# A Swin block on one core: normalized tokens transposed by SyncE's transfers, dense tokens, maxima in a row-maximum bank, first scores later

## The reference, cut to what matters

```
xn  = layernorm(x) * g1 + b1
xw  = roll(xn, (-3, -3)) cut into 7x7 windows              # 1024 windows of 49 tokens
q, k, v = xw @ qkv_w + qkv_b                               # per head
p   = softmax(q * 8**-0.5 @ k.T + position_bias + window_mask)
x1  = x + roll back((p @ v) @ proj_w + proj_b)
out = x1 + gelu(layernorm(x1) * g2 + b2 @ fc1_w + fc1_b) @ fc2_w + fc2_b
```

## Time and profile before

| | |
|---|---|
| timed runs, median | 1094.67 us |
| profiled execution | 1094.25 us, span 1092.5 us |
| attention stage, about | 55 to 833 us of the span |
| MLP stage, about | 853 to 1092 us of the span |
| busy, share of the span | PE 87%, DVE 82%, ACT 71%, POOL 69% |
| mean granted TensorE clock | 0.988 of full speed |

### The profile page before, as it was taken

One profiled execution on the slowest core, in us unless ns is written; L12 is line 12 of the kernel. 1 busy time (PEld: TensorE's weight loads), 2 busy tenths in 40 slices (PEclk: granted clock), 3 DMA queues, 4 the chain that ended last, 5 costly groups with the idle time before them and its releaser, 6 DMA issues. The chain is left out here.

```text
span 1092.5 us, 45511 instructions
## 1 busy us (share of the span) xinstructions
PE 946.4 (87%) x16004; PEld 750.9 (69%) x16004; DVE 891.7 (82%) x2021; ACT 773.7 (71%) x1733; POOL 751.6 (69%) x971
## 2 busy tenths in 40 slices
PE   0489999999999999999999999999983688888887
PEld 0268887888788878887888788887873355554555
DVE  5678888888888888888888888898975677777776
ACT  0368888888888888888888888888863444444544
POOL 6258888888888888888888888888865444444441
PEclk9999999999999999999999999999996899999999
DMA  1022222222222222222222222232220343444444
GB/s 54 22 72 74 67 74 72 64 65 75 73 62 65 74 72 63 65 76 73 61 65 75 73 62 66 75 75 64 64 62 1 69 96 91 97 96 92 98 93 96
DMA packets 139237, 77.32 MB, mean 71 GB/s; under 512 B 105923, under 2 KB 138980, under 8 KB 139190
## 3 DMA queue, kind: packets, MB, share of 16 engines
q1 hardware_dynamic: 86966, 63.83, 22.3%
q10 hardware_dynamic: 52224, 12.85, 6.1%
HBM read 10.48 MB, written 9.63 MB: 18 GB/s over the span
## 5 line engine op out<-in xcount | busy, mean ns | idle before, releaser
L405 POOL TENSOR_TENSOR pl<-p 113x294 f16<-113x294 f32 x512 | 347.7, 690 | 46.6 <-ACT p L476 34.9
L476 ACT ACTIVATE p<-banks 113x294 f32<-113x294 f32 x512 | 214.8, 420 | 48.1 <-PE banks L655 41.0
L639 PE MATMUL banks<-Qh,KAg 128*128 128x147 f16 x2048 | 217.8, 228 | 0.0
L801 DVE TENSOR_REDUCE rowmax<-banks 113x12 f32<-113x588 f32 x256 | 192.5, 752 | 10.2 <-PE banks L622 8.3
L639 PEld LDWEIGHTS banks<-Qh,KAg 128*128 128x128 f16 x2048 | 166.5, 97 | 30.9
L1115 DVE TENSOR_TENSOR gl<-gel 128x448 f16<-128x448 f32 (+1 forms) x192 | 123.9, 647 | 64.2 <-ACT gel L1015 64.1
L655 PE MATMUL banks<-Vb,p 113*128 113x36 f16 x3072 | 175.3, 180 | 0.9 <-POOL pl L405 0.9
L608 PE MATMUL banks<-bs_h,idt 113*128 113x294 f16 x512 | 146.4, 293 | 31.3 <-DVE QAg L795 25.4
L655 PE MATMUL banks<-Vb,pl 113*128 113x36 f16 x1536 | 162.7, 180 | 0.0
L655 PEld LDWEIGHTS banks<-Vb,p 113*128 113x128 bf16 x3072 | 156.1, 97 | 1.1 <-POOL pl L405 1.1
L245 POOL TENSOR_TENSOR rstd<-var,mhalf 112x7 f32<-112x7 f32 x64 | 95.3, 1489 | 83.7 <-ACT var L240 83.7
(11 more groups left out here) (140 smaller groups left out, 2664.8 us busy)
## 6 DMA issues: line engine op xcount, KB each, us to landing
Qh<-QAB SPq DMA_DIRECT2D x192, 98.0 KB, 2.2
Vb<-Vn SPq DMA_DIRECT2D x256, 54.0 KB, 2.1
xres<-in_x SPq DMA_DIRECT2D x64, 147.0 KB, 2.2
KAh<-KA SPq DMA_DIRECT2D x192, 49.0 KB, 1.9
out_y<-ybuf SPq DMA_DIRECT2D x64, 147.0 KB, 2.1
Qh<-mT SPq DMA_DIRECT2D x128, 4.6 KB, 2.2
hT<-xtok ACTq DMA_TRANSPOSE x32, 2.8
hT<-htok ACTq DMA_TRANSPOSE x32, 2.7
```

The lines of the kernel that those rows point to most:

```text
L405: nc.gpsimd.tensor_tensor(pl[p % 4][:, :, :, 0:N].rearrange("p a w n -> p (a w) n"), p32[p % 4][:, :, :, 0:N].rearrange("p a w n -> p (a w ...
L476: nc.scalar.activation(p32[p % 4][:, :, :, 0:N].rearrange("p a w n -> p w a n"), src, ACT.Exp, scale=1.0 / SB).then_inc(s_exp, 1)
L639: i = nc.tensor.matmul(bank[:, w * COLS:(w + 1) * COLS], KAg[upar][:, 2 * p + w, :, :].rearrange("p g n -> p (g n)"), Qh[upar][:, level, : ...
L801: nc.vector.tensor_reduce(rowmax[:, 2 * p:2 * p + 4, :].rearrange("p (k w) a -> p k (w a)", k=2), sc[0:AP_, :, 0:2 * COLS].rearrange("p k ...
```

## The change

- `xtok` becomes a pair of buffers. The seven TensorE transposes and ScalarE's copy into `xT` are removed; SyncE issues one transposing transfer from `xtok` to `xT`, after a wait for the low half of the tokens. That wait stands before the last of the three `Qh` transfers, the transfer behind it and before those of `Vb`.
- `xT` is dense: 49 columns a window, no padding. V then lies on 49 partitions a window, and the `Vb` transfers carry 49 rows instead of 64.
- The maxima are transposed into free columns of the second `sc` bank (`psM`) instead of `aux`. Their wait for the low half of V moves to the transposes of the outputs, which now come before the second scores; the second scores wait for `mT`.
- The first scores of the next unit come after one more transposed-score pair and one value product.
- In the MLP the transposing transfer goes from ScalarE's queue to SyncE's, behind two halves of the store of the unit before. `htok` is the same pair as `xtok`.

```diff
-        xtok = sb("xtok", [PT, CH, FULL], f16)
+        xtok = [sb(f"xtok{i}", [PT, CH, FULL], f16) for i in range(2)]
+        psM = banks[2].bitcast(f16)[:, 6 * FULL:6 * FULL + AP_]
...
+        def landed(u, par):
+            return 8 * (u - par) + 16
+
+        def ln_high(act, u, par, n):
             act.wait_ge(s_xn, n)
-            wait(act, s_xtp, n - 1)
+            if exists(u - 2):
+                act.wait_ge(s_xT[par], landed(u - 2, par))
...
-        def x_transposes(pe, n):
-            pe.wait_ge(s_xlo, n)
-            for c in range(CH):
-                i = nc.tensor.transpose(psT[:, c * PT:(c + 1) * PT], xtok[:, c, :], idt[0:PT, 0:PT])
-            i.then_inc(s_xtp, 1)
...
-        xT = [sba(f"xT{i}", [HL, UW, GP], f16) for i in range(2)]
+        xT = [sba(f"xT{i}", [FULL, TOK + FULL - 2 * N], f16) for i in range(2)]
...   (SyncE, attention)
                     for hp in range(HP):
+                        if hp == HP - 1 and exists(t + 2):
+                            sp.wait_ge(s_xlo, t + 3)
                         sp.dma_start(Qh[par][hp:ROWS:HP, :, hp, :, :], QAB[par][hp:ROWS:HP, :, :, :]).then_inc(s_tb[par], 16)
+                elif exists(t + 2):
+                    sp.wait_ge(s_xlo, t + 3)
+                if exists(t + 2):
+                    sp.dma_start_transpose(xT[par][:, 0:TOK].rearrange("p (c n) -> p c n", n=PT),
+                                           xtok[par][:, :, :].rearrange("p c n -> p (c n)")).then_inc(s_xT[par], 16)
+                if exists(t):
                     wait(sp, s_pv, PAIRS * done(t - 2))
                     for w in range(2):
                         for g in range(G):
-                            sp.dma_start(Vb[par][g * GP:(g + 1) * GP, :, w, g, :],
-                                         Vn[par][w * GP:(w + 1) * GP, :, g, :, :].rearrange("p l a d -> p l (a d)"))\
+                            sp.dma_start(Vb[par][g * GP:g * GP + N, :, w, g, :],
+                                         Vn[par][w * N:(w + 1) * N, :, g, :, :].rearrange("p l a d -> p l (a d)"))\
...   (ScalarE, attention)
-                if exists(t + 2):
-                    act.wait_ge(s_xtp, done(t + 2))
-                    nc.scalar.activation(xT[par][:, :, 0:N], psT[0:HL, 0:TOK].rearrange("p (w n) -> p w n", n=N),
-                                         ACT.Copy).then_inc(s_xT, 1)
...   (TensorE, attention)
                 def k_piece(j):
                     if j == 0:
-                        pe.wait_ge(s_xT, done(t + 1))
+                        pe.wait_ge(s_xT[new], landed(t + 1, new))
...
                 def v_piece():
-                    if exists(t + 2):
-                        pe.wait_ge(s_xT, done(t + 2))
-                    else:
-                        pe.wait_ge(s_qlow, 2 * (t + 1) + 1)
+                    pe.wait_ge(s_qlow, 2 * (t + 1) + 1)
...
                 if exists(t - 1):
                     pe.wait_ge(s_m16, done(t - 1))
+                    nc.tensor.transpose(psM, m16[:, :], idt[0:AP_, 0:AP_]).then_inc(s_mtp, 1)
+                if exists(t + 1):
+                    k_piece(0)
+                if exists(t - 3):
+                    pe.wait_ge(s_olo, done(t - 3))
                     if exists(t):
                         pe.wait_ge(s_vlow, done(t))
                     else:
                         wait(pe, s_OT, done(t - 4))
-                    nc.tensor.transpose(psT[:, 0:AP_], m16[:, :], idt[0:AP_, 0:AP_]).then_inc(s_mtp, 1)
-                if exists(t + 1):
-                    k_piece(0)
-                if exists(t):
-                    scores(t, par, 1)
-                if exists(t - 3):
-                    pe.wait_ge(s_olo, done(t - 3))
-                    wait(pe, s_mT, done(t - 1))
...
                     for k in range(PAIRS):
                         i = nc.tensor.transpose(psT[:, k * FULL:k * FULL + AP_], otok[:, k, :], idt[0:AP_, 0:AP_])
                     i.then_inc(s_otp, 1)
+                if exists(t):
+                    wait(pe, s_mT, done(t - 1))
+                    scores(t, par, 1)
...
-                if exists(t + 2):
-                    if exists(t + 1):
-                        pe.wait_ge(s_qlow, 2 * (t + 1) + 1)
-                    x_transposes(pe, t + 3)
...
                     t_scores(t - 1, new, 4)
-                if exists(t + 1):
-                    scores(t + 1, new, 0)
-                if exists(t - 1):
                     t_scores(t - 1, new, 5)
                     pv(t - 1, new, 1)
+                if exists(t + 1):
+                    scores(t + 1, new, 0)
+                if exists(t - 1):
                     pv(t - 1, new, 2)
...   (SyncE, MLP)
+                def store(half):
+                    cols = slice(half * CH * C // 2, (half + 1) * CH * C // 2)
+                    sp.dma_start(out[bass.ds(t - 1, 1), :, cols].rearrange("u p n -> p (u n)"),
+                                 ybuf[1 - par][:, cols]).then_inc(s_store[1 - par], 16)
+
                 if exists(t - 1):
                     sp.wait_ge(s_yo, done(t - 1))
-                    sp.dma_start(out[bass.ds(t - 1, 1), :, :].rearrange("u p n -> p (u n)"),
-                                 ybuf[1 - par][:, :]).then_inc(s_store[1 - par], 16)
+                    store(0)
+                elif exists(t):
+                    sp.wait_ge(s_h, 3 * done(t))
+                if exists(t + 2):
+                    sp.wait_ge(s_mlo, done(t + 2))
+                if exists(t - 1):
+                    store(1)
+                if exists(t + 2):
+                    sp.dma_start_transpose(hT[par][:, :, :], htok[par][:, :, :].rearrange("p c n -> p (c n)"))\
+                      .then_inc(s_hT[par], 16)
...   (ScalarE, MLP)
-                if exists(t + 2):
-                    act.wait_ge(s_mlo, done(t + 2))
                 if exists(t):
                     gelu(2)
-                if exists(t + 2):
-                    act.dma_start_transpose(hT[par][:, :, :], htok[par][:, :, :].rearrange("p c n -> p (c n)"))\
-                      .then_inc(s_hT[par], 16)
```

More of the change, by code:

```diff
@@ L145, in swin_block_kernel @@
         s_xlo = sem("x_low_ready")
-        s_xtp = sem("x_transposed")
-        s_xT = sem("xT_ready")
+        s_xT = [sem(f"x_transposed{i}") for i in range(2)]
         s_kfull = sem("k_projected")
@@ L467, in v_high @@
                         act.wait_ge(s_vb[new], v_blocks_of(t - 1, new))
-                    nc.scalar.activation(Vn[new][:, 0, :, :, 0:HD].rearrange("p g a d -> p (g a) d"),
-                                         aux[:, 0:PAIRS * C].rearrange("p (a d) -> p a d", d=HD), ACT.Copy,
+                    nc.scalar.activation(Vn[new][0:2 * N, 0, :, :, 0:HD].rearrange("p g a d -> p (g a) d"),
+                                         aux[0:2 * N, 0:PAIRS * C].rearrange("p (a d) -> p a d", d=HD), ACT.Copy,
                                          scale=SV / (SX * SWT)).then_inc(s_vhigh, 1)
@@ L515, in step @@
                 if exists(t + 2):
-                    ln_high(act, t + 3)
+                    ln_high(act, t + 2, par, t + 3)
                 if exists(t - 1):
@@ L553, in project @@
                 def project(bank, col, j):
-                    tok = xT[new][:, 8 * j:8 * j + 8, 0:N]
+                    tok = xT[new][0:HL, j * HALF:(j + 1) * HALF]
                     nc.tensor.matmul(bank[:, 0:HALF], wh[:, col:col + FULL], tok, start=True, stop=False)
@@ L664, in step @@
                         wait(pe, s_OT, done(t - 4))
-                    nc.tensor.transpose(psT[:, 0:AP_], m16[:, :], idt[0:AP_, 0:AP_]).then_inc(s_mtp, 1)
-                if exists(t + 1):
-                    k_piece(0)
-                if exists(t):
-                    scores(t, par, 1)
-                if exists(t - 3):
-                    pe.wait_ge(s_olo, done(t - 3))
-                    wait(pe, s_mT, done(t - 1))
-                    if not exists(t - 1):
-                        wait(pe, s_OT, done(t - 4))
                     for k in range(PAIRS):
@@ L723, in step @@
                     t_scores(t - 1, new, 4)
+                    t_scores(t - 1, new, 5)
+                    pv(t - 1, new, 1)
                 if exists(t + 1):
@@ L726, in step @@
                 if exists(t - 1):
-                    t_scores(t - 1, new, 5)
-                    pv(t - 1, new, 1)
                     pv(t - 1, new, 2)
@@ L747, in _ @@
             for k in xT:
-                nc.vector.memset(k[:, :, :], 0.0)
+                nc.vector.memset(k[:, TOK:TOK + FULL - 2 * N], 0.0)
             for k in Vn:
-                link(nc.vector.memset(k[:, :, :, :, HD:CP], 0.0))
-                for w in range(2):
-                    nc.vector.memset(k[w * GP:w * GP + N, 0, :, :, HD:CP], SV / SO)
-            nc.vector.memset(xtok[:, :, 2 * C:HL], SX)
-            nc.vector.memset(xtok[:, :, HL:FULL], 0.0)
+                nc.vector.memset(k[:, 1, :, :, HD:CP], 0.0)
+                nc.vector.memset(k[:, 0, :, :, HD:CP], SV / SO)
+            for k in xtok:
```

(10 more changed lines are left out.)

19 lines of the change are left out of this document (8 added, 11 removed).

## The result

| | before | after |
|---|---|---|
| timed runs (4 each), median (range) | 1094.84 us (1093.88 to 1096.41) | 1146.13 us (1144.32 to 1148.94) |
| profiled execution, span | 1094.25, 1092.5 us | 1146.5, 1144.7 us |
| mean granted TensorE clock | 0.988 | 0.958 |
| attention step, mean of 63 | 12.02 us | 12.37 us |
| MLP, start of the first to start of the last matmul of line 1052 | 231.9 us | 261.7 us |

The change made the kernel slower: ratio 1.0474, 95% interval 1.0456 to 1.0492. The prediction was 1068 us, faster; it was wrong in sign. Of the 51 us lost, 63 × 0.35 = 22 lie in the attention stage and 30 in the MLP.

What follows compares the result with a forecast made beforehand. Attention bound by a loop through VectorE's wait for the transposed row maxima, the MLP by a chain of waits through ScalarE's GELUs and transfer. 1094.25 − 33 + 7 = 1068 us; own range 1055 to 1080.

Steps and rivals of the forecast that it cites:

- the term of −33 us: Attention: first scores later lets mT start earlier, 0.55 us a step for 60 steps; bounds −30 to −37.
- the rows of maxima start as now: Attention, SyncE's queue: the rows still issue near 409.55 though mT is ready earlier; slack 0.6 us, so no cost.
- unless the issue takes over 1.8 us: Attention, SyncE's queue: the transposing transfer's issue, taken as 1.23 us, delays the maxima's rows only beyond this length.
- a later landing: Attention: Vb on 7 DMA engines instead of 16 would land later, which the step of slack hides.
- price of nothing: Attention: first row maximum about 0.35 us later against mT, absorbed by VectorE's 0.29 us idle before the K low half.
- the bounds: Attention, o-transposes ahead of second scores: a cost between 0 and +0.3 us a step, +18 us.
- a wait takes mT's place: Rival, attention: the gap moves to the first row maxima (+18 us) or the K projection; 1086 us, chance 0.16.
- slower: Rival, both stages: transposing transfer lands late behind SyncE's other transfers; 1136 us at a 3.8 us landing; chance 0.16.
- The MLP's loop: MLP: two-unit loop through ybuf, two stores, transfer, matmuls, GELU and splits; 7.61 us, 3.80 a unit against 3.70.
- the estimate gave 0.74: MLP loop, SyncE: two store issues of 0.32 us with about 0.1 of registers and waits between.
- +7: MLP: the loop adds 0.10 us a unit over 64 units, +7 us; bounds −43 and +20.

Runs made afterwards that it cites:

- e10: e7 with the V transfers at 64 rows a group instead of 49: 1048.28 us, ratio 0.9589 to the kernel before.
- e9: Changed kernel with the second scores ahead of the transposes of the outputs again: 1148.60 us, ratio 1.0494 to the kernel before.
- e3: Changed kernel with the four V transfers moved into the next step, behind its rows of maxima: 1117.33 us, ratio 1.0212 to the kernel before.
- e7: Changed kernel with the edits of e3 and e9, and SyncE's MLP stores those of two units back: 1063.68 us, ratio 0.9705 to the kernel before.
- e6: Changed kernel with four extra matmuls an MLP step ahead of TensorE's wait for the transposed tokens: 1131.89 us, ratio 1.0354 to the kernel before.
- e1: Changed kernel with the MLP's transposing transfer back on ScalarE's queue and the store one transfer: 1120.49 us, ratio 1.0242 to the kernel before.

## Why the prediction was wrong

- **mT and the first scores: right, and covered.** VectorE's wait for mT is down to 1.3 us and TensorE's for QAg to 1.6 us over the whole span. The step of 12.02 − 0.52 = 11.50 us that the term of −33 us stands for is what e10 measured, once SyncE's queue no longer held it. That the two agree to 0.01 is in part luck: in e10 VectorE still waits 35 us for row maxima.
- **The step that failed: "the rows of maxima start as now".** The prediction gave SyncE 4.98 us from the end of the low half of the tokens to the rows of maxima (404.57 to 409.55), with 0.6 us of slack. Measured: 400.09 to 406.46, 6.37 us. The V transfers, priced at 2.6 us from the earlier trace rows, where each carries 64 rows, take 3.36 (+0.76); behind them lie two gaps between instructions, 0.25 and 0.41 us, where the sum had 0.1 in all (+0.56); the transposing transfer to the next issue takes 1.34 instead of 1.2 (+0.14); the third Q transfer took 0.07 less. That is 1.39 us; less the slack of 0.6, 0.79 a step, and the step came out 0.87 above 11.50. In time: 63 × 0.87 = 55 of the 78 us by which the prediction missed. The clause "unless the issue takes over 1.8 us" watched the issue of the transposing transfer, which takes 1.30 against 1.23. SyncE's queue used to wait for mT before it issued the rows, 49.9 us in all, so its gaps and small growth cost nothing; the edit that freed mT turned this queue into the loop. One of the gaps could be read beforehand: in the kernel before, the load starts 0.32 us behind the end of the V transfers (405.28 + 2.61 = 407.89):

```profile
408.21 0.34 SPq L350 DMA_DIRECT2D xres<-in_x  x1
```

- **49 rows.** The prediction named the smaller V transfers and looked at their landing; the price was on SyncE's queue. The Trainium skill (*DMA: Bandwidth & Descriptors*, section on why a DMA increments its semaphore by 16), by which fewer DMA engines carry 49 rows, was cited there for a later landing and for load on those engines, not for a price on SyncE's queue. The same section says that the issuing sequencer itself writes the part of the semaphore's 16 that unused engines don't post. That would be work on SyncE for every such transfer, and agrees in direction with 0.82 against 0.63 us; no run here shows on how many engines a transfer ran, and no third number of rows was tried, so the cause of the longer issue stays open.
- **O-transposes ahead of the second scores.** The first row maximum starts 1.04 us behind mT instead of 0.61: +0.43, predicted 0.35. Its price of nothing held in the changed kernel (e9), for another reason than the one given: it lay beside the longer loop. Between e3 and e7 it was worth 0.20 a step, inside the bounds. The rival "a wait takes mT's place" named this wait and that of the K projection. Both are there (58.1 and 22.8 us), but the loop ran through a third that it did not name, that for the rows of maxima.
- **The transposing transfer.** It lands after 2.8/2.9/4.6 us (least, median, most) in the attention stage and 2.7/2.8/4.1 in the MLP, against 2.8 and at most 3.1 predicted; only 5 of the 128 transfers take more than 3.1. So the "slower" rival, which needed a late landing, came near the measured time (1136) by luck: its mechanism is not what the runs show.
- **The MLP's loop: right, but short in one term, and the clock was missing.** 7.61 us was written; 7.82 and 7.61 were measured where the clock was full, and 7.76 on average in e6. The term that was too small is the two stores with what lies between them: 0.93 us from the first store's issue to the transfer's (964.05 to 964.98), where the estimate gave 0.74. For the stage at full clock that is +15 us (247.3 in e6 against 231.9), where +7 was predicted; some 3 of them also stand in e1, where ScalarE issues the transfer. The other 14 us are TensorE's clock, which the prediction did not price at all: in the loop the engine stands up to 1.43 us for a transfer, the clock falls from 2.4 to 1.2 GHz in parts of the stage, and the matmuls of lines 1052 to 1075, slower, enter the loop themselves. That this is the cause is shown by e6: with part of the wait filled, the clock stays at 1.00 and the 14 us are gone. How much standing it takes is not shown. TensorE was idle for 18 of 100 us before and for 19 in the changed kernel; before, no single wait between 920 and 1000 us was longer than 0.84 us, and the clock stayed at 1.00.

With both losses mended nothing of the slowdown is left: in e10 the step is the predicted 11.50, the MLP takes 214.6 us, and the kernel is 46 us faster than before. The remainder of 3 us between e1's MLP and that of before (235.1 and 231.9) was not looked into.

## What to carry to other kernels

When an edit frees the wait that closes a loop, write down the next loop with every queue in it, instruction by instruction, gaps included; a transfer queue that waits in it hides what its own length will cost. A wait's total in the profile says nothing of its worth until it is known to lie on the loop: here 32 us of it vanished for nothing, and 0.7 us a step on SyncE's queue were worth 28. Before a stage is allowed to become bound by a loop through a transfer, ask what the matrix engine's granted clock will do while the engine stands.

## What the runs showed of the hardware that had not been expected

- A transfer of 49 rows a group (41.3 KB) holds SyncE's queue for 0.82 us, one of 64 rows (54.0 KB) for 0.63 us, in the same place of the same program.
- In the MLP of the changed kernel the granted clock fell to a mean of 0.93 and 0.83 over stretches of 100 and 92 us, though TensorE was idle hardly longer than before. In the loop shown above, with the clock at half, the 42 matmuls of line 1075 took 1.72 us instead of 1.16. Four more matmuls a step brought the clock back to 1.00 and made the kernel 14 us faster.
- The transposing transfer lands at the same median of 2.8 us from SyncE's queue as from ScalarE's, with two stores issued right in front of it.
